# Two orders changed in a gated slot-attention kernel: GpSimd's low halves at a change of head, and one filter tap on VectorE

## What is computed

```python
def short_conv(x, w):                       # 4 taps along time
    y = sum(xp[:, i:i + t] * w[:, i] for i in range(K))
    return jax.nn.silu(y)
q = short_conv(h @ Wq, cq); k = short_conv(h @ Wk, ck)
v = short_conv(h @ Wv, cv); w = l2norm(short_conv(h @ Ww, cv))
g = jax.nn.log_sigmoid(h @ Wf1 @ Wf2)
...
def step(carry, xs):                        # over time
    Sk = Sk * gt[:, :, None, :] + k_t[..., :, None] * bw[:, :, None, :]
    Sv = Sv * gt[..., None] + bw[..., None] * v_t[:, :, None, :]
    s = jnp.einsum('bhd,bhdm->bhm', q_t, Sk) * SCALE
    a = jax.nn.softmax(s, axis=-1)
    o_t = jnp.einsum('bhm,bhmd->bhd', a, Sv)
```

## Time and profile before

| | us |
|---|---|
| median of 3 runs | 1989.41 |
| lowest and highest | 1987.39, 1990.56 |
| the profiled execution | 1987.3 |
| its span | 1985.6 |
| TensorE busy | 1921.0 (97%) |
| VectorE busy | 1774.2 (89%) |
| GpSimd busy | 1333.7 (67%) |
| ScalarE busy | 1395.3 (70%) |

### The profile page before, as it was taken

How to read it: one execution, slowest core, us unless ns; L and a number is a source line. 1 busy time by engine, 2 the same in 40 slices (tenths; PEclk the granted TensorE clock), 3 DMA queues, 4 the chain that set the end, 5 groups by cost and what they waited for, 6 DMA issues and landing times.

```text
span 1985.6 us, 41492 instructions
## 1 busy us (share of the span) xinstructions
PE 1921.0 (97%) x12192; PEld 1623.8 (82%) x12192; DVE 1774.2 (89%) x4096; ACT 1395.3 (70%) x3986; POOL 1333.7 (67%) x2289
## 2 busy tenths in 40 slices
PE   7999999999999999999999999999999999999897
PEld 5778888888888888888888888888888888887776
DVE  5699999999999999999999999999999999998587
ACT  4467777777777777777777777777777777777543
POOL 5376676777677676767677676767677676766444
PEclk8899999999999999999999999999999999999899
DMA  3021111111111111111111110111111110112300
GB/s 78 1 61 21 27 34 24 26 24 33 26 24 27 27 34 20 30 24 33 27 24 26 27 35 15 36 24 33 23 27 26 24 37 14 25 22 43 63 22 33
DMA packets 53645, 58.51 MB, mean 29 GB/s; under 512 B 14896, under 2 KB 44720, under 8 KB 53424
## 3 DMA queue, kind: packets, MB, share of 16 engines
q0 software_dynamic: 9216, 33.56, 11.5%
q1 hardware_dynamic: 44208, 22.29, 4.1%
HBM read 20.19 MB, written 37.75 MB: 29 GB/s over the span
## 4 chain that ended last, share of the span: by engine, by line
PE 85%; POOL 7%; DVE 4%; issue 2%; ACT 1%; DMA 0%; POOLq 0%; DVEq 0%; ACTq 0%
PE proj_ps L722 15%; PE mix_ps L806 11%; PE V_ps L777 10%; PE work_ps L931 8%; PE work_ps L937 7%; PE tr_ps L746 6%; PE V_ps L755 5%; PE work_ps L1608 5%; PE proj_ps L397 4%; PE work_ps L826 3%; PE mix_ps L813 2%; POOL w_lo L370 2%; PE tr_ps L786 2%; PE work_ps L828 2%; PE proj_ps L1479 1%
## 5 line engine op out<-in xcount | busy, mean ns | idle before, releaser
L591 DVE SCALAR_TENSOR_TENSOR conv<-proj_ps,coefs,conv 128x511 f32<-128x511 f32 (+2 forms) x768 | 561.2, 731 | 9.9 <-ACT conv L347 3.0
L298 POOL TENSOR_TENSOR W<-W,tot 128x256 f32<-128x256 f32 x384 | 256.0, 667 | 245.3 <-PE mix_ps L806 245.1
L1059 POOL TENSOR_TENSOR A_lev<-A,masks 128x256 f32<-128x256 f32 x448 | 319.2, 717 | 0.1
L806 PE MATMUL mix_ps<-W,U 128*128 128x128 f32 x1792 | 294.6, 286 | 9.8 <-POOL W L298 4.3
L777 PE MATMUL V_ps<-A_lev,UT 128*128 128x128 f32 x1792 | 286.6, 283 | 1.4 <-DVE V_ps L687 1.4
L806 PEld LDWEIGHTS mix_ps<-W,U 128*128 128x128 f32 x1792 | 256.2, 192 | 35.7 <-issue 20.2
L715 DVE COPY_PREDICATED A<-masks,mix_ps 128x256 f32<-128x256 uint32 x448 | 268.5, 599 | 6.6 <-PE mix_ps L806 6.5
L584 DVE TENSOR_TENSOR wT<-wT,tot 128x128 f32<-128x128 f32 x768 | 233.2, 343 | 40.3 <-DVE U L567 1.8
L777 PEld LDWEIGHTS V_ps<-A_lev,UT 128*128 128x128 f32 x1792 | 238.0, 193 | 23.2 <-DVE V_ps L687 23.0
L356 ACT ACTIVATE th<-conv 128x512 f32<-128x512 f32 x256 | 162.3, 634 | 104.3 <-DVE conv L591 103.3
L722 PE MATMUL proj_ps<-hT_hi,w_hi 128*128 128x512 f32 x512 | 222.2, 434 | 4.2 <-DVE conv L591 2.4
(11 more groups left out here) (204 smaller groups left out, 4763.2 us busy)
## 6 DMA issues: line engine op xcount, KB each, us to landing
head_sum<-y_sb POOLq DMA_DIRECT2D x64, 512.0 KB, 6.5
w_raw<-in_L_attn_Ww SPq DMA_DIRECT2D x16, 128.0 KB, 2.2
w_raw<-in_L_attn_Wq SPq DMA_DIRECT2D x16, 128.0 KB, 2.2
w_raw<-in_L_attn_Wk SPq DMA_DIRECT2D x16, 128.0 KB, 2.3
w_raw<-in_L_attn_Wv SPq DMA_DIRECT2D x16, 128.0 KB, 2.2
wo_raw<-in_L_attn_Wo SPq DMA_DIRECT2D x16, 128.0 KB, 2.0
head_sum<-in_L_attn_hidden_states SPq DMA_DIRECT2D x1, 2048.0 KB, 10.0
acc<-head_sum SPq DMA_DIRECT2D x4, 512.0 KB, 3.8
```

The costliest lines, as they stand in the source:

```text
L298: nc.gpsimd.tensor_tensor(w, w, block_tot(u3.par, lev, 0), ALU.mult).then_inc(W_step, 1)
L591: nc.vector.scalar_tensor_tensor(y_, proj_ps[:, CONV_BANK[i], 0:T - back], filt(u, i, KW - 1 - back), y_, ALU.mult, ALU.add).then_inc(conv ...
L806: last = nc.tensor.matmul(mix_ps[:, half, p * P:(p + 1) * P], Ulev(u3, lev)[:, p * P:(p + 1) * P], after_odd(W[:, p * T // 2:(p + 1) * T / ...
L1059: nc.gpsimd.tensor_tensor(dst, diag_after_odd(lev), mask_cols(lev), ALU.mult)\
```

## The change

Two edits. In GpSimd's list the low halves for the gate, for q and for k go from ahead of the gate products to behind k's silu; the low half for w stays. In VectorE's list the second tap of w goes from ahead of the first mixing to behind V's second level, directly ahead of the third tap.

```diff
@@ -1094,15 +1094,16 @@
                 if s.next_h:
                     low_weights(pool, s.next_h, 0)
-                    low_f(pool, s.next_h)
-                    low_weights(pool, s.next_h, 1)
-                    low_weights(pool, s.next_h, 2)
                 if u1 and u1.h and u1.par == 0:
                     low_weights(pool, u1.h, 3)
                 if u1:
                     for lv in range(4, LEVELS - 1):
                         gate_products(pool, u1, lv)
                     silu_qk(pool, u1, 2)
+                if s.next_h:
+                    low_f(pool, s.next_h)
+                    low_weights(pool, s.next_h, 1)
+                    low_weights(pool, s.next_h, 2)
@@ -1321,7 +1322,6 @@
                 if u1:
                     conv_tap(dve, u1, 0, 0)
-                    conv_tap(dve, u1, 0, 1)
                 if u3:
                     mixable(dve, u3, 0)
                     mix(dve, 0)
@@ -1330,6 +1330,7 @@
                 if u2:
                     descend(dve, u2, 1)
                 if u1:
+                    conv_tap(dve, u1, 0, 1)
                     conv_tap(dve, u1, 0, 2)
```

## The result

The changed kernel took 2039.6 us (median of 4 runs, 2036.9 to 2041.6) where the kernel before took 1990.0 on the same chip (1987.4 to 1991.2): a ratio of 1.025, 95% interval 1.0236 to 1.0264. The forecast was 2035, slower, with 2014 to 2053 as the range. The profiled execution's span is 2039.8 us against 1985.6.

What follows compares the result with a forecast made beforehand. The prediction took TensorE, busy 97% of the span, as the bound. 1987.3 us profiled, plus 21.6 for the tap and 25.5 for the changes of head, made 2034.4, forecast as 2035 with range 2014 to 2053.

Steps and rivals of the forecast that it cites:

- What bounds: TensorE, busy 97% of the span: a change counts only where it shortens or lengthens TensorE's own list.
- The gain at `key_query`: Behind a change of head, TensorE's wait for k's silu goes: 0.36 us each, 15 times, 5.4 us if nothing else is late.
- The tap, 0.46 a slot: Second tap behind L681 starts q's projection 0.82 later against 0.36 of cover: 0.46 us a slot, 21.6 us in 47 slots.
- The hold at a change of head: GpSimd's five long instructions hold VectorE's five behind L544; with the tap, 1.1 to 1.7 us each, 25.5 us for 15.
- The 1.34: Behind a change of head, `U_top` ends 1.34 us later because GpSimd's run holds VectorE's instructions of levels 3 and 4.
- the meeting with L298: Behind the first mixing product, GpSimd's L298 holds a VectorE multiplication of level 6: 0 to 0.6 us, taken as 0.6.
- Lock or shared bandwidth: VectorE and GpSimd exclude each other for whole instructions (1.34 us later) or share bandwidth (0.9, sum some 7 us lower).
- Rival B: In every slot GpSimd's L298 and L1059 hold v's silu: up to 0.3 us more, up to 2053 us; chance 0.13.
- Rival A: Only one cost exists: change of head alone 2005 to 2010 us, tap alone 2016 to 2018; chance 0.18.
- C: Tap free and VectorE's delay at `U_top` under 0.51 us: 5.4 us won, 1984 us; chance 0.06.

Runs made afterwards that it cites:

- one-column kernel: Low halves for gate, q and k behind k's silu, those three on one column per block, taps unmoved, against the kernel before: 1996.2 us, ratio 1.0029.

## Why the prediction was right, point by point

- **What bounds.** TensorE's list, and both edits reach it through VectorE: confirmed by both new waits.
- **The gain at `key_query`.** The wait for `qk` went in all 15 slots. From L937 to the first mixing product it is now 1070.88 - 1069.11 = 1.77, as in an ordinary slot, so the 0.36 came, and TensorE spent it waiting for `U_top`. Confirmed.
- **The tap, 0.46 a slot.** 1.84 in place of 1.37 behind L681, 28.44 to 28.49 in place of 28.00. Confirmed, and its sign on the other side, three taps ahead, as well.
- **The hold at a change of head, 1.1 to 1.7.** 1.53 (29.86 - 28.33). Five instructions for five, ending 0.16 behind GpSimd's run, was forecast and is what the rows show; the one-column kernel shows that the cause is the hold. From L544 to `U_top` it is 1073.10 - 1066.65 = 6.45 in place of 1041.29 - 1036.63 = 4.66, thus 1.79 more, where I had 1.34 and 0.6. The 1.34 was right: the meeting with L298 took 0.96 - 0.49 = 0.47, and the rest is 1.32. I took 1.7 where 1.53 was measured: 2.6 us too much in the sum. A little of it is my subtraction: 1.34 and 1.94 less 0.74 are 0.60 and 1.20, where I wrote 0.66 and 1.27.
- **Lock or shared bandwidth.** I had put 0.9 against 1.34 between them, and 1.32 was measured, which speaks for the lock. A pair of multiplications that takes 0.49 alone takes 1.54 held, three times as much, where sharing would at most double it. But my reading of the row was off: the 0.71 of the held copy isn't 0.29 plus the rest of GpSimd's instruction, which was 1039.24 - 1038.69 = 0.55 and would make 0.84. It is the rest plus 0.16, and the sum used this 0.16 (as 0.15), so nothing in it hangs on the slip.
- **Rival B**, a second hold in every slot: not there. L687 isn't what TensorE waits for, and ordinary slots have only the tap's 0.46.
- **Rival A**, one of the two costs isn't there, fell with the two edits alone, 1.0131 and 1.0148; **C**, faster, with the result.
- **What the sum lacked.** The granted clock: four stretches of the lower level, about 5.3 us, in none of my cases. For the profiled execution, 2034.4 - 2.6 + 5.7 + 4 = 2041.5, and it took 2041.55. It is the slowest of the four; their median, 2039.6, is 4.6 above the forecast. The fastest, 2036.9, has a mean granted clock of 0.986 where the profiled one has 0.982, so it probably had fewer such stretches, which no trace of it shows. The prediction spoke of idle TensorE only as time lost in the wait itself. That the sum came within 5 us is in part luck: what was too much and what was missing have opposite signs.

## What to carry to other kernels

Before a block of work is moved off the path that one engine waits on, look at what the other engine does at the new place: here GpSimd's long instructions were harmless beside VectorE's taps from PSUM and beside its idle time, and a run of them of 3.4 us put off `U_top` by 1.3 us beside short SBUF-to-SBUF instructions. And for a step with a wait on either side of it, take both covers from the trace. Ahead of L681 there was 0.16 us (0.78 less the 0.62 that a third tap ahead cost), behind it 0.36: a tap of 0.78 costs in either direction.

## What the runs showed of the hardware that I hadn't expected

**The granted clock falls in a kernel whose TensorE is 96% busy.** In the changed kernel it fell at 4 of 15 changes of head, in the two others in which TensorE waits about 0.9 us for `U_top` at 5 and 4 of 15, at a cost of 0.6 to 1.4 us each (from the distances). In the kernels without that wait it fell at no change of head, even where in each slot the matmuls stand still for 1.0 us ahead of q's projection. So a standstill of that length isn't enough by itself; the place is part of it. The wait for `U_top` isn't needed either: in the one-column kernel the clock fell at 107 us, while the pipeline fills, and the slot was 1.4 longer. TensorE had idled 0.92 and 0.88 us just before; it did the same there in the kernel with the low halves in the next slot, whose clock held. Which places fall, and what besides the idle time decides it, no run here tells.

**How VectorE is held.** Held instructions end some 0.15 behind the end of GpSimd's, one of VectorE's for one of GpSimd's, for as long as GpSimd's run lasts. The Trainium skill, page "SBUF — State Buffer", section "SBUF: two separate sides", describes it as an exclusive lock for the whole instruction. The rows agree: in the changed kernel's run the first pair of L584 ends 0.15 behind k's silu (1068.80 and 1068.65), the copy 0.15 behind the gate's low half (1069.27 and 1069.12), the second pair 0.16 behind the last. So does the one-column kernel, with 0.32 for the copy of level 4 beside a GpSimd instruction of 0.25, and 0.44 beside one of 0.52.
